# Layer norms' statistics, centred tokens and residual in two sets of SBUF buffers instead of columns of z's PSUM bank

## The chip, the cores and the metric

The kernel runs on one core of a Trainium2 chip. The core's engines are TensorE (PE, matrix products and transposes), VectorE (DVE), ScalarE (ACT), GpSimd (POOL) and SyncE (SP, which here only issues transfers); each runs its own queue in order and waits on semaphores. The metric is the device time of one execution in microseconds.

## What is computed

One layer of a small language model on 2 x 2048 tokens: a gather of 64 columns of an embedding table, a layer norm, a block of two selective scans (one forward, one backward in time), and a layer of 32 experts of which each token takes one. Cut to what matters:

```python
h = table[:, 192:256][x]                       # tokens 2 x 2048, 64 channels
a = attn(layernorm(h)); h = h + a              # attn normalises once more and adds its own input
h = h + experts(layernorm(h))

def attn(x):                                   # 64 channels in, 128 inside
    c, gate = split((layernorm(x) * g + b) @ in_w.T)
    act = silu(conv4(c))
    fwd, bwd = mamba(act), flip(mamba(flip(act)))
    return concat(fwd, bwd) * silu(gate) @ out_w.T + x

def mamba(u):                                  # per direction
    x, z = split(u @ in_w.T); x = silu(conv4(x))
    dt = softplus(...x...); B, C = 16 columns each of x @ xproj_w.T
    h_t = h_{t-1} * exp(dt * A) + dt * x * B;  y = sum_n h_t * C + x * D   # 16 states per channel
    return y * silu(z) @ out_w.T
```

## The kernel before

Tokens are cut into 8 chunks of 512. A *unit* is one chunk in one direction; there are 16, numbered 0 to 15, eight for each row of the batch (four forward, then four backward). A unit's scan has 16 states, held as four groups r = 0 to 3 of four quarters q, so a unit is 16 scans over 512 steps, at *places* p = 0 to 15 of the unit (r = p // 4). All engines run the loop `for u in range(UNITS)` in an order written out by hand: DVE and ACT have a function `between(u, p)` each, which says what stands behind scan or decay p; PE has one list per unit.

The work of a unit is divided as follows:

- ACT makes the decays exp(dt A) in three PSUM banks in turn (L979), at most three scans ahead of DVE, and the softplus (L955 to L968) of the unit two further on.
- DVE scans (L1336). It also forms the input products of groups 1 and 3, dt x times a row of B that PE spreads into a PSUM bank (L1323), each of 2048 columns.
- POOL forms the input products of groups 0 and 2 from SBUF operands (L454, called B(u,r) below), multiplies every group of scanned states by C, also from SBUF (L463, called C(u,r)), and ends the softplus of unit u+2 in three instructions (L440, L443, L447). All its operands are in SBUF. Its order in unit u is C(u-1,3), B(u,2), C(u,0), softplus, C(u,1), B(u+1,0), C(u,2). C(u,r) waits for scan 4r+3 of the unit (by the semaphore `scanned`), B(u+1,0) for PE's fold of C(u,0).
- PE folds the products by C into y (L639), spreads B, and does the other products.

Layer norms are done on DVE and ACT between scans. `norm_first`/`norm_sum` add up the channels (L1230); `norm_centre` subtracts the mean (L1234, into `xc`); ACT squares (L908, `sq`); `norm_var` sums the squares and forms the variance with one or two TENSOR_SCALARs (L1239 to L1242); ACT takes its logarithm and an exponential (L913, L915, into `lnr`); `norm_newton` corrects the inverse root in three small instructions (L1250 to L1252), each with a wait on the one before; `scaled` multiplies `xc` by it (L1255). Sums, squares, variance and Newton's values stand in columns 384 to 415 of PSUM bank `ZED`. There is one `xc`.

There are sixteen norms. Norms 0 to 7 are those of the gathered chunks; each has two results, `u2d` twice over (the input of the in-projection, `start_u2`) and the once-normed tokens, which `start_residual` builds in columns 0 to 255 of bank `ZED` and adds to `x0` (L1270). Norms 0 to 3 run in the prologue. Norm 4+k is begun at place 15 of unit k and goes on in unit k+1 (k = 0 to 3): `norm_var` at place 0, Newton and `start_u2` at place 1, `start_residual` at place 12. Norms 8 to 15 are those ahead of the experts, with the one result `xf`. Four are begun at place 15 of units 5, 7, 9, 11 (the table `ENDS`) and go on in units 6, 8, 10, 12; three (`QUICK`, chunks of units 12 to 14) run inside units 13 to 15; the last runs after the loop.

Bank `ZED` also takes, once per unit, PE's product z for three units ahead (`zed`, L592, read by ACT in L949), and the experts' logits. Therefore `norm_first` waits until ACT has read z (`z_ready`) and until the expert of the chunk before is chosen (`choice_ready`), and PE's `zed` waits for `u_added`.

## Time and profile before

| | |
|---|---|
| median of 3 runs | 615.37 us |
| lowest, highest | 614.62, 620.71 us |
| the profiled execution | 620.66 us, its span 618.9 us |
| POOL busy | 517.5 us (84%) |
| DVE busy | 484.0 us (78%) |
| PE busy, ACT busy | 451.6 us, 356.2 us |
| the 16 x 16 scans on DVE (L1336) | 235.1 + 78.1 us, 1267 ns each |
| POOL's products, by C and by B | 284.5 + 140.4 us, 4.53 us each |
| granted TensorE clock, mean | 0.817 |

The loop begins at about 80 us, and POOL's last product ends at 578; what follows is the last two chunks' experts, on PE, ACT and DVE. A timeline row gives an instruction's start from the span's start, its length and, in brackets, how long its engine had been idle before it and what released it. "x2" merges neighbours.

### The profile page before, as it was taken

What the parts mean: (1) busy time and instruction counts of PE and PEld (TensorE: products, weight loads), DVE (VectorE), ACT (ScalarE), POOL (GpSimd) and SP (SyncE); (2) the same over time, 40 slices, a digit from 0 to 9 for tenths busy, and PEclk for the clock granted to TensorE, in tenths of its full rate; (3) what the DMA queues carried; (4) which work ended last, traced back from release to release, by engine and by line L of the source; (5) the groups of instructions that cost most, each with busy time, mean ns of one, the idle gap of its engine ahead of it and who ended that gap; (6) DMA issues with size and microseconds to landing.
All of it is one profiled execution on the core that took longest, in us unless ns stands there. A gap on an engine that the chain in (4) does not pass through costs nothing.

```text
span 618.9 us, 5369 instructions
## 1 busy us (share of the span) xinstructions
PE 451.6 (73%) x1485; PEld 160.7 (26%) x1485; DVE 484.0 (78%) x600; ACT 356.2 (58%) x634; POOL 517.5 (84%) x190
## 2 busy tenths in 40 slices
PE   2476756577777777778796887777777765777887
PEld 1222212132222221313141323132313221323332
DVE  3433069898989897989699989898989898899720
ACT  2354565757575757474748494849484944555222
POOL 5727159999999999999989999999999999897100
PEclk9887957787878787869787987898779876879856
DMA  6829358846464646563716772667276726400000
GB/s 66 33 30 181 79 138 205 190 136 142 136 143 129 149 135 137 141 143 107 171 50 144 175 171 73 171 152 167 70 168 163 162 68 160 87 10 1 8 4 14
DMA packets 51072, 71.31 MB, mean 115 GB/s; under 512 B 16434, under 2 KB 17378, under 8 KB 51042
## 3 DMA queue, kind: packets, MB, share of 16 engines
q1 hardware_dynamic: 48050, 69.63, 46.6%
q0 software_dynamic: 1024, 1.05, 4.4%
q10 hardware_dynamic: 1968, 0.29, 0.3%
q8 instruction: 12, 0.20, 0.2%
q14 instruction: 18, 0.15, 0.1%
HBM read 60.45 MB, written 10.49 MB: 115 GB/s over the span
## 4 chain that ended last, share of the span: by engine, by line
POOL 38%; issue 26%; PE 17%; DVE 10%; ACT 5%; ACTq 1%; another core or an unknown queue 1%; POOLq 0%; DVEq 0%
POOL st L463 20%; POOL st L454 13%; DVE st L1336 5%; PE ps L725 3%; POOL l_ L440 2%; POOL dt L443 2%; DVE st L1323 2%; PE ps L741 2%; PE ps L639 2%; PE ps L579 2%; PE ps L651 1%; ACTq L893 1%; PE ps L626 1%; PE ps L558 1%; PE ps L724 1%
## 5 line engine op out<-in xcount | busy, mean ns | idle before, releaser
L463 POOL TENSOR_TENSOR st<-st,repC 128x2048 f32<-128x2048 f32 x63 | 284.5, 4526 | 10.3 <-ACT carry L985 7.0
L1336 DVE TENSOR_TENSOR_SCAN st<-ps,carry,st 128x512 f32<-128x512 f32 x192 | 235.1, 1267 | 20.1 <-ACT carry L985 12.0
L979 ACT ACTIVATE ps<-dtS,negA 128x512 f32<-128x512 f32 x256 | 169.1, 680 | 53.5 <-DVE st L1336 52.1
L454 POOL TENSOR_TENSOR st<-duS,repB 128x2048 f32<-128x2048 f32 x31 | 140.4, 4529 | 0.0
L639 PE MATMUL ps<-st,fold 128*32 128x512 f32 x504 | 83.7, 742 | 74.1 <-POOL st L463 74.0
L1336 DVE TENSOR_TENSOR_SCAN st<-ps,zero,st 128x512 f32<-128x512 f32 x64 | 78.1, 1266 | 3.1 <-ACT ps L979 2.9
L1323 DVE TENSOR_TENSOR st<-duS,ps 128x2048 f32<-128x2048 f32 x33 | 74.9, 2271 | 3.6 <-PE ps L626 3.2
L579 PE MATMUL ps<-act,wT 128*128 128x512 f32 x128 | 64.3, 648 | 5.2 <-issue 5.2
L985 ACT ACTIVATE carry<-st 128x4 f32<-128x4 f32 x48 | 9.8, 205 | 77.3 <-DVE st L1336 77.1
L626 PE MATMUL ps<-xr,Bw 128*128 128x512 f32 x66 | 48.9, 833 | 6.8 <-DVE lnr L1316 6.0
L440 POOL TENSOR_TENSOR l_<-l_,e_ 128x512 f32<-128x512 f32 x16 | 20.4, 1276 | 29.8 <-DVE e_ L1274 29.8
L639 PEld LDWEIGHTS ps<-st,fold 128*32 128x32 f32 x504 | 10.8, 117 | 122.7 <-POOL st L463 114.1
L428 POOL DMA_INDIRECT x<-in_L_tok_ple_table,idx x32 | 30.5, 952 | 12.5 <-issue 9.3
L725 PE MATMUL ps<-xfT,w 64*128 64x512 f32 x64 | 40.5, 718 | 0.0
L579 PEld LDWEIGHTS ps<-act,wT 128*128 128x128 f32 x128 | 26.2, 212 | 38.2 <-issue 37.4
L1012 ACT ACTIVATE tall<-ps,b 128x512 f32<-128x512 f32 x32 | 21.7, 678 | 22.0 <-PE ps L725 21.8
L609 PE MATMUL ps<-xr,wT 128*32 128x512 f32 x32 | 25.5, 893 | 11.5 <-DVE st L1323 11.4
L600 PE MATMUL ps<-xr,dtproj 128*128 128x512 f32 x32 | 23.3, 818 | 13.7 <-ACT xr L942 13.5
L1274 DVE SCALAR_TENSOR_TENSOR e_<-ps,e_ 128x512 f32<-128x512 f32 x16 | 10.7, 669 | 23.7 <-ACT l_ L968 23.7
L741 PE MATMUL ps<-tall,w 128*64 128x256 f32 x128 | 22.8, 516 | 8.3 <-ACT tall L1012 8.3
L651 PE MATMUL ps<-zr,wT 128*128 128x512 f32 x32 | 25.6, 892 | 1.2 <-DVE zr L1342 1.2
L884 ACT ACT_TABLE_LOAD x16 | 20.5, 1283 | 9.7 <-issue 9.5
(126 smaller groups left out, 579.4 us busy)
## 6 DMA issues: line engine op xcount, KB each, us to landing
dtS<-dt_dram SPq DMA_DIRECT2D x64, 256.0 KB, 7.2
duS<-du_dram SPq DMA_DIRECT2D x64, 256.0 KB, 4.8
repC<-bc_dram SPq DMA_DIRECT2D x64, 256.0 KB, 5.7
repB<-bc_dram SPq DMA_DIRECT2D x60, 128.0 KB, 2.8
dt_dram<-dt SPq DMA_DIRECT2D x16, 256.0 KB
du_dram<-du SPq DMA_DIRECT2D x16, 256.0 KB
bc_dram<-bc_sb SPq DMA_DIRECT2D x16, 64.0 KB, 5.5
out_h<-fin SPq DMA_DIRECT2D x8, 128.0 KB, 2.1
```

What stands on the lines that cost most here:

```text
L440: pool.tensor_tensor(l_[:], l_[:], e_[:], ALU.subtract).then_inc(sem("sp_log1p"), 1)
L454: pool.tensor_tensor(st[:, r], duS[:, u % 2], row, ALU.mult).then_inc(sem("dbu_pool"), 1)
L463: pool.tensor_tensor(st[:, r], st[:, r], row, ALU.mult).then_inc(sem("hc_ready"), 1)
L579: mm = pe.matmul(ps[:, bank, :], conv_wT(way(u), k), act_at(u, 6 - k if way(u) else k), start=(k == 0), stop=(k == 3))
L626: pe.matmul(ps[:, SHORT, :], Bw[:, way(u), r, :], x_of(u), start=True, stop=True) \
L639: mm = pe.matmul(ps[32 * q:32 * q + 32, Y, :], fold[:], st[:, r, q], start=False, stop=(r == NR - 1), skip_group_check=True)
L651: pe.matmul(ps[:, SHORT, :], wT[:, 12 + way(u), :], z_of(u), start=True, stop=True) \
L725: pe.matmul(ps[:, bank, :], w1[:, 8 * k:8 * k + 8, :].rearrange("p e h -> p (e h)"), xfT[0:DM, :], start=False, stop=True).then_inc(sem("h ...
L741: mm = pe.matmul(ps[DM * h:DM * h + DM, bank, 0:T // 2], w, src, start=(k == 0), stop=(k == NBLK), skip_group_check=True)
L979: sc.activation(decay_bank(u, r, q), dtS[:, u % 2, q], ACT.Exp, scale=negA[:, way(u), q, r:r + 1]).then_inc(sem("decay_ready"), 1)
L1323: dve.tensor_tensor(st[:, r], duS[:, u % 2], row, ALU.mult).then_inc(sem("dbu_dve"), 1)
L1336: dve.tensor_tensor_scan(st[:, r, q, order], decay_bank(u, r, q)[:, order], st[:, r, q, order], first, ALU.mult, ALU.add).then_inc(sem("sc ...
```

## The change

The statistics get an SBUF tile `stats` with two sets of 32 columns; `xc` and `lnr` (now `lnrs`) get two sets as well; norm n uses set n % 2. The once-normed tokens of chunks 0 to 7 are built in `fin`, the SBUF tile that the kernel's output leaves from later on. Bank `ZED` then no longer holds anything of a norm, and the waits for it go: DVE's on `z_ready` and `choice_ready`, PE's on `u_added`.

```diff
+        lnrs = sb("lnrs", [P, 2, 2, 2 * TC])
+        stats = sb("stats", [P, 2, 32])
-        xc = sb("xc", [P, TC, DM])
+        xc = sb("xc", [P, 2, TC, DM])
...
-        sum_ps = ps[:, ZED, 384:384 + TC]
-        ss_ps = ps[:, ZED, 388:388 + TC]
-        var_ps = ps[:, ZED, 392:400]
-        nt_ps = ps[:, ZED, 400:408]
-        ny_ps = ps[:, ZED, 408:416]
+        def stat(n, at, width):
+            return stats[:, n % 2, at:at + width]
...
             def zed(u, bank):
                 if bank == ZED:
-                    if norm_b(u - 3) is not None and norm_b(u - 3) < NCH:
-                        pe.wait_ge(sem("u_added"), norm_b(u - 3) + 1)
...
-                dve.scalar_tensor_tensor(xc[:], wide(sum_ps), -1.0 / DM, src, ALU.mult, ALU.add) \
+                dve.scalar_tensor_tensor(xc[:, n % 2], wide(stat(n, 0, TC)), -1.0 / DM, src, ALU.mult, ALU.add) \
...
-                    ch.step(dve.tensor_scalar(var_ps[:, TC:], ss_ps, (1.0 + EPS) / DM, EPS * EPS, ALU.mult, ALU.add))
+                    ch.step(dve.tensor_scalar(stat(n, 8 + TC, TC), stat(n, 4, TC), (1.0 + EPS) / DM, EPS * EPS,
+                                              ALU.mult, ALU.add))
...
-                ch.step(dve.tensor_tensor(nt_ps[:, 0:w], var_ps[:, 0:w], r, ALU.mult))
+                ch.step(dve.tensor_tensor(stat(n, 16, w), stat(n, 8, w), r, ALU.mult))
...
-            def scaled(dst, k):
-                return dve.scalar_tensor_tensor(dst, xc[:], -0.5, wide(ny_ps[:, TC * k:TC * k + TC]),
+            def scaled(n, dst, k):
+                return dve.scalar_tensor_tensor(dst, xc[:, n % 2], -0.5, wide(stat(n, 24 + TC * k, TC)),
...
-                ch.step(scaled(u_ps, 0))
+                ch.step(scaled(n, fin[:], 0))
                 src = x0_of(TC * n)
-                dve.tensor_tensor(src, u_ps, src, ALU.add).then_inc(sem("u_added"), 1)
+                dve.tensor_tensor(src, fin[:], src, ALU.add).then_inc(sem("u_added"), 1)
...
-                    dve.wait_ge(sem("z_ready"), n - CB + 4)
...
-                    wait(dve, "choice_ready", n - NCH)
-                    dve.wait_ge(sem("z_ready"), min(BEGINS[n - NCH] + 4, UNITS))
```

Beside that, the hand-written orders of DVE, ACT and PE are new in many places: on DVE the residual (p 12 to 1), `normed` of units 6, 8, 10, 12 (p 3 to 2), input product 3 (p 11 to 10), the expert's choice (p 6 and 7 to p 7 and 9), and in units 13 to 15 the centring (p 7 to 8) and Newton's step (p 12 to 11); on ACT the softplus (in p 0 to 1, its exponential and sum p 0 and 3 to 6, its logarithm p 4 to 7); on PE the folds and experts' products within the unit. POOL's and SP's queues are the same.

The same stretch of DVE's queue in unit 2, from Newton's step to the scans behind it; `st<-ps,carry,st` is a scan. Before:

```order
L1250 TENSOR_TENSOR ps<-ps,lnr 128x8
L1251 TENSOR_TENSOR ps<-ps,lnr 128x8
L1252 SCALAR_TENSOR_TENSOR ps<-ps,lnr 128x8
L1255 SCALAR_TENSOR_TENSOR u2d<-xc,ps 128x4x64 x2
L1336 SCALAR_TENSOR_TENSOR st<-ps,carry,st 128x512 x2
```

and the residual, ten scans later in the same unit:

```order
L1336 SCALAR_TENSOR_TENSOR st<-ps,carry,st 128x512
L1255 SCALAR_TENSOR_TENSOR ps<-xc,ps 128x256
L1270 TENSOR_TENSOR x<-ps,x 128x256
L1336 SCALAR_TENSOR_TENSOR st<-ps,carry,st 128x512 x3
```

The same place after the change (its `x<-fin,x` is the residual's add):

```order
L1250 TENSOR_TENSOR stats<-stats,lnrs 128x8
L1251 TENSOR_TENSOR stats<-stats,lnrs 128x8
L1252 SCALAR_TENSOR_TENSOR stats<-stats,lnrs 128x8
L1255 SCALAR_TENSOR_TENSOR u2d<-xc,stats 128x4x64 x2
L1255 SCALAR_TENSOR_TENSOR fin<-xc,stats 128x256
L1268 TENSOR_TENSOR x<-fin,x 128x256
L1334 SCALAR_TENSOR_TENSOR st<-ps,carry,st 128x512 x2
```

The operands called `ps` are now `stats` and `fin`, and the residual's two instructions moved ahead of the two scans.

DVE's queue in unit 13, from the norm's sum to the scans behind Newton's step, before:

```order
L1230 TENSOR_REDUCE ps<-x 128x4
L1234 SCALAR_TENSOR_TENSOR xc<-ps,x 128x256
L1336 SCALAR_TENSOR_TENSOR st<-ps,carry,st 128x512 x4
L1323 TENSOR_TENSOR st<-duS,ps 128x2048
L1239 TENSOR_REDUCE ps<-sq 128x4
L1242 TENSOR_SCALAR ps<-ps 128x4
L1336 SCALAR_TENSOR_TENSOR st<-ps,carry,st 128x512
L1250 TENSOR_TENSOR ps<-ps,lnr 128x4
L1251 TENSOR_TENSOR ps<-ps,lnr 128x4
L1252 SCALAR_TENSOR_TENSOR ps<-ps,lnr 128x4
L1336 SCALAR_TENSOR_TENSOR st<-ps,carry,st 128x512
L1255 SCALAR_TENSOR_TENSOR xf<-xc,ps 128x256
```

and with the change:

```order
L1229 TENSOR_REDUCE stats<-x 128x4
L1334 SCALAR_TENSOR_TENSOR st<-ps,carry,st 128x512 x2
L1233 SCALAR_TENSOR_TENSOR xc<-stats,x 128x256
L1334 SCALAR_TENSOR_TENSOR st<-ps,carry,st 128x512 x2
L1321 TENSOR_TENSOR st<-duS,ps 128x2048
L1238 TENSOR_REDUCE stats<-sq 128x4
L1242 TENSOR_SCALAR stats<-stats 128x4
L1334 SCALAR_TENSOR_TENSOR st<-ps,carry,st 128x512
L1250 TENSOR_TENSOR stats<-stats,lnrs 128x4
L1251 TENSOR_TENSOR stats<-stats,lnrs 128x4
L1252 SCALAR_TENSOR_TENSOR stats<-stats,lnrs 128x4
L1334 SCALAR_TENSOR_TENSOR st<-ps,carry,st 128x512 x2
```

The sum comes one scan earlier and the centring one scan later; the input product, the variance and Newton's step come one scan earlier, and the copy `xf` has two scans between Newton's step and itself instead of one.

## Rows read from the trace of the kernel before

**Rows 1.** The page: busy time by engine; then the chain that ended last, by engine.

```profile
PE 451.6 (73%) x1485; PEld 160.7 (26%) x1485; DVE 484.0 (78%) x600; ACT 356.2 (58%) x634; POOL 517.5 (84%) x190
...
POOL 38%; issue 26%; PE 17%; DVE 10%; ACT 5%; ACTq 1%; another core or an unknown queue 1%; POOLq 0%; DVEq 0%
```

**Rows 2.** Waits of all engines: who waited for whom, us in total, times, longest.

```profile
PEld ps L639 <- POOL st L463: 114.1, 49, 6.0
...
POOL l_ L440 <- DVE e_ L1274: 29.8, 3, 16.6
...
POOL st L463 <- ACT carry L985: 7.0, 3, 4.4
...
POOL st L494 <- DVE st L1336: 3.9, 1, 3.9
...
POOL st L463 <- DVE st L1336: 3.3, 2, 2.3
```

**Rows 3.** POOL's timeline (start us, us, instruction), units 1 and 2, and unit 7.

```profile
141.37 9.00 POOL L463 TENSOR_TENSOR st<-st,repC 128x2048 f32<-128x2048 f32 x2
150.34 4.53 POOL L454 TENSOR_TENSOR st<-duS,repB 128x2048 f32<-128x2048 f32 x1
154.82 4.52 POOL L463 TENSOR_TENSOR st<-st,repC 128x2048 f32<-128x2048 f32 x1
...
315.30 1.28 POOL L440 TENSOR_TENSOR l_<-l_,e_ 128x512 f32<-128x512 f32 x1 [1.84 <-DVE e_ L1274]
```

**Rows 4.** DVE's timeline (same columns), end of unit 1 and start of unit 2.

```profile
141.43 0.42 DVE L1234 SCALAR_TENSOR_TENSOR xc<-ps,x 128x256 f32<-128x256 f32 x1
143.44 1.28 DVE L1336 TENSOR_TENSOR_SCAN st<-ps,carry,st 128x512 f32<-128x512 f32 x1 [1.58 <-ACT ps L979]
...
145.39 2.29 DVE L1323 TENSOR_TENSOR st<-duS,ps 128x2048 f32<-128x2048 f32 x1
147.59 1.28 DVE L1336 TENSOR_TENSOR_SCAN st<-ps,carry,st 128x512 f32<-128x512 f32 x1
148.78 0.16 DVE L1250 TENSOR_TENSOR ps<-ps,lnr 128x8 f32<-128x8 f32 x1
...
149.39 0.87 DVE L1255 SCALAR_TENSOR_TENSOR u2d<-xc,ps 128x256 f32<-128x256 f32 x2
150.19 2.45 DVE L1336 TENSOR_TENSOR_SCAN st<-ps,carry,st 128x512 f32<-128x512 f32 x2
```

**Rows 5.** POOL's timeline, end of unit 7 and start of unit 8.

```profile
328.20 9.02 POOL L463 TENSOR_TENSOR st<-st,repC 128x2048 f32<-128x2048 f32 x2
337.16 4.54 POOL L454 TENSOR_TENSOR st<-duS,repB 128x2048 f32<-128x2048 f32 x1
341.64 4.54 POOL L463 TENSOR_TENSOR st<-st,repC 128x2048 f32<-128x2048 f32 x1
```

**Rows 6.** DVE's timeline, end of unit 7 and scans of unit 8.

```profile
329.28 0.42 DVE L1234 SCALAR_TENSOR_TENSOR xc<-ps,x 128x256 f32<-128x256 f32 x1
...
338.50 0.40 DVE L1255 SCALAR_TENSOR_TENSOR xf<-xc,ps 128x256 f32<-128x256 f32 x1
```

**Rows 7.** DVE's line 1476 by duration, min/median/max; then POOL's timeline beside it.

```profile
L1476 DVE TENSOR_TENSOR st<-st,repC x3: 679/679/1576, 577.2 to 579.3; 128x512 f32<-128x512 f32 x3
...
576.94 1.28 POOL L494 TENSOR_TENSOR st<-st,repC 128x512 f32<-128x512 f32 x1 [3.90 <-DVE st L1336]
```

**Rows 8.** DVE's groups at the start, each shape apart: busy us, mean ns.

```profile
L1198 DVE TENSOR_TENSOR st<-st 32x128 f32<-32x128 f32 x1 | 0.3, 280 | 0.0
L1197 DVE TENSOR_SCALAR st<-st 32x128 f32<-32x128 f32 x1 | 0.2, 218 | 0.0
```

**Rows 9.** POOL's timeline in unit 13.

```profile
508.69 4.54 POOL L454 TENSOR_TENSOR st<-duS,repB 128x2048 f32<-128x2048 f32 x1
513.18 9.00 POOL L463 TENSOR_TENSOR st<-st,repC 128x2048 f32<-128x2048 f32 x2
```

**Rows 10.** POOL's timeline, first softplus.

```profile
42.21 1.27 POOL L440 TENSOR_TENSOR l_<-l_,e_ 128x512 f32<-128x512 f32 x1 [11.37 <-DVE e_ L1274]
```

More of the change, by code:

```diff
@@ L816, in _ @@
                     partial(u - 1)
+                if 1 <= u <= CB:
+                    x_chunk(CB + u - 1, LONG)
+                if third:
+                    experts_out(ENDS[u - 2])
                 if u - 2 in QUICK:
@@ L837, in _ @@
                 if u - 2 in QUICK:
-                    experts_out(u - 2)
+                    hidden(u - 2, 3)
+                if second:
+                    turn_choice(ENDS[u - 1])
+                if u + 3 < UNITS:
+                    zed(u + 3, ZED)
                 if third:
                     turn_back(ENDS[u - 2])
-                if u + 3 < UNITS:
-                    zed(u + 3, ZED)
+                if u - 2 in QUICK:
+                    experts_out(u - 2)
                 if 1 <= u <= CB:
@@ L907, in squares @@
                 sc.wait_ge(sem("centred"), n + 1)
-                sc.activation(sq[:], xc[:], ACT.Square).then_inc(sem("squared"), 1)
+                sc.activation(sq[:], xc[:, n % 2], ACT.Square).then_inc(sem("squared"), 1)
             def rsqrt(n):
@@ L1065, in between @@
                         keep_last(u, 0)
+                if p == 6:
+                    if u + 2 < UNITS:
+                        softplus_exp(u + 2)
+                    if u + 2 < UNITS:
+                        softplus_plus1(u + 2)
                     if u - 2 in ENDS:
                         hidden_relu(ENDS[u - 2], 3)
-                if p == 6:
+                    if 1 <= u <= CB:
+                        uT_chunk(CB + u - 1)
+                if p == 7:
+                    if u + 2 < UNITS:
+                        softplus_ln(u + 2)
                     if u - 1 in ENDS:
@@ L1238, in norm_var @@
                 dve.wait_ge(sem("squared"), n + 1)
-                ch.step(dve.tensor_reduce(ss_ps, sq[:], AX, ALU.add))
+                ch.step(dve.tensor_reduce(stat(n, 4, TC), sq[:], AX, ALU.add))
                 if n < NCH:
-                    ch.step(dve.tensor_scalar(var_ps[:, TC:], ss_ps, (1.0 + EPS) / DM, EPS * EPS, ALU.mult, ALU.add))
-                dve.tensor_scalar(var_ps[:, 0:TC], ss_ps, 1.0 / DM, EPS, ALU.mult, ALU.add) \
+                    ch.step(dve.tensor_scalar(stat(n, 8 + TC, TC), stat(n, 4, TC), (1.0 + EPS) / DM, EPS * EPS,
+                                              ALU.mult, ALU.add))
+                dve.tensor_scalar(stat(n, 8, TC), stat(n, 4, TC), 1.0 / DM, EPS, ALU.mult, ALU.add) \
                    .then_inc(sem("ln_var"), 1)
@@ L1406, in between @@
                         input_product(u, 1)
-                    if is_unit(u) and 2 in on_dve(u):
-                        input_product(u, 2)
                     if u - 2 in QUICK:
@@ L1484, in _ @@
             norm_first(NCH + nth(last), x0_of(tile0(last)))
-            norm_centre(x0_of(tile0(last)))
+            norm_centre(NCH + nth(last), x0_of(tile0(last)))
             norm_var(NCH + nth(last))
```

151 lines of the change are left out of this document (69 added, 82 removed).

## The prediction

> **What bounds the kernel now.** I read four views. The page comes first: POOL is busy for 517.5 us and DVE for 484.0 us of 618.9, and the chain that ended last runs for 38% of the span through POOL, more than through any other engine [rows 1]. POOL's own waits come next: 29.8 us ahead of the softplus, of which only 1.84 us lie inside the loop (at 315.30, in unit 7), and 7.0, 3.9 and 3.3 us, all in the first unit and the last two [rows 2, 3]. POOL's timeline shows the same thing from inside: in units 1 to 13 each instruction starts where the last one ends, 4.5 us apart: the pair at 141.37 fills 9.00 us and B(2,2) follows at 150.34 [rows 3]. So whatever makes POOL idle in those units is lost for good. DVE's timeline, last, shows how little room there is: in unit 2 its scan number 3 ends at 152.6 and POOL takes the product that needs it, C(2,0), at 154.82 [rows 3, 4]. In unit 8 the pair is 338.5 and 341.64 [rows 5, 6]. DVE leads POOL by two to three microseconds, no more.
>
> **A look at what DVE's operands are.** In the loop of the kernel before, no DVE instruction reads two tensors from SBUF: one of the two is always in PSUM. The one exception stands after the loop: L1476, SBUF times SBUF. Its three instances take 679, 679 and 1576 ns; the first starts at 577.2 and the last at 579.3, so the long one is the first (two short ones ahead of it would put the last at 578.6). It starts while POOL's L494 (also SBUF times SBUF) runs from 576.94 to 578.22. It ends at 578.8, some 0.55 us after POOL's; the two behind it meet an idle POOL and take 679 [rows 7]. My reading: a DVE instruction with two SBUF inputs is held until the POOL instruction that is reading SBUF has ended.
>
> **The change part by part.** Every norm's intermediate moves to SBUF. These DVE instructions now have two SBUF inputs: the centring, the three of Newton's step, and each scaled copy (one for the experts' norms; two for u2d, one and the add for the residual of chunks 4 to 7). A norm's TENSOR_SCALARs now go from SBUF to SBUF with one input. The nearest rows are at the start: an immediate TENSOR_SCALAR on 32x128 in SBUF takes 218 ns, the two-input TENSOR_TENSOR of the same size 280 [rows 8]. It gets through its columns in less time than one input stream gives the other, so I take it to use the second input path too, and to be held. POOL's instructions in the loop all read SBUF and take 4.5 us. I work out three kinds of norm against the old time axis; what counts is when the next POOL instruction that needs a scan can start.
>
> *Chunks 4 to 7, units 1 to 4.* In unit 2 the centring arrives at 141.43, with POOL in C(1,2), and then the two TENSOR_SCALARs, each with a wait on the one before. The first ends with C(1,3) at 150.34, the second with B(2,2) at 154.82 [rows 3, 4]. C(2,0) needs four scans, so POOL now stands still and nothing holds DVE any longer. Behind the second TENSOR_SCALAR lie the product 2.2, a scan 1.2, Newton 0.6, u2d 0.8, the residual, which the change moves here from later in the unit, 0.8 (two instructions of u2d's size), and two scans 2.4: 8.0, with the TENSOR_SCALAR itself 8.2 us, by which C(2,0) is late [rows 4]. Four units: 33. If one-input instructions are not held, the first wait is Newton's, to the same 154.82, and 0.6 + 0.8 + 0.8 + 2.4 = 4.6 is left, or 18 for four.
>
> *Experts' norms in units 6, 8, 10, 12.* In unit 8 the centring (329.28) waits for C(7,2), the TENSOR_SCALAR for C(7,3) to 337.16, then 3.4 for product and scan, and Newton's first waits for B(8,2), to 341.64 [rows 5, 6]. After it: Newton 0.6, a scan 1.2, the xf copy 0.4 (moved up one scan), a scan 1.2: C(8,0) is 3.4 late. Four units: 14.
>
> *Units 13 to 15.* The centring stands one scan later than before, Newton's step behind scan 11. By then both B(14,0) and C(13,2) are ready for POOL, so its first instruction ends with B at 513.18 and its second with C(13,2) at 517.67; four scans and the xf copy, 5.4, then hold up C(13,3) [rows 9]. In unit 14 the same gives about 4.4, since POOL idles already. In unit 15 POOL works with gaps and DVE is the bound, so each hold counts: about 4 at the centring and 4 at Newton's. Sum 18.
>
> *Prologue.* Chunk 2's norm meets the three 1.27 us instructions of the first softplus, from 42.21 on, at its TENSOR_SCALARs and at Newton's step; it loses two of their lengths, 2.5 [rows 10]. The gathers that stand around it are no compute instructions; I cost them at nothing, and up to 5 if they hold DVE as well. The last norm runs when POOL has finished: nothing.
>
> *What I cost at nothing.* The waits that are dropped (on z, on the expert's choice, PE's on u_added) stood ahead of a POOL that never paused, so their going frees nothing that sets the end. The new order on PE is covered by its 114.1 us of waits for POOL's products [rows 2]. One place there is a new wait: in units 1 to 4 the transposes of u2d now stand ahead of the fold of C(u-1,3). If u2d is late, that fold and DVE's y times z behind it are late too; in between lie the residual and two scans, 3.2 us, for four transposes and one fold, and I take that as enough. ACT's softplus moves from places 0 to 4 to places 1 to 7, nearer to the DVE step that POOL waits for ahead of its own softplus. POOL waited there once in the loop, 1.84 us [rows 3]; where the cover is gone I allow as much again in each of units 1 to 4, 7 us for the upper bound, and nothing in the sum. An operand in SBUF instead of PSUM saves little: xf, written to SBUF, takes 0.40, and the centring 0.42 [rows 6]. SP's queue is the same.
>
> **The sum.** 33 + 14 + 18 + 2.5 = 67.5, of which 15 hang on the one-input instructions (without them 53). The profiled execution took 620.66 us (span 618.9), the median of the runs is 615.37; I add to the median: 683 us, or 668 without them. Either side of that, leads that DVE rebuilds and holds that find POOL idle make 655 to 705.
>
> The Trainium skill (SBUF — State Buffer, section "Who interferes with whom") says this outright: a DVE instruction with two SBUF inputs contends with a GpSimd one that reads SBUF, as does a tensor_scalar in its two-port mode, and the second to issue blocks until the first ends. The trace agrees with its 1576 ns against 679. By that rule the sum is the higher one of the two above; by the 1576 ns alone, a row that shows no one-input instruction beside POOL, it is the lower one.
>
> **Rivals.**
> *DVE starves.* POOL's next instruction starts before the last is quite over: the pair at 141.37 ends at 150.37, B(2,2) starts at 150.34 [rows 3]. If it takes its turn ahead of the held DVE instruction, DVE waits until POOL runs dry. Then unit 2's centring goes at 154.82, and 10.3 us of DVE's work (from 141.43 to 152.6, less its idle 1.58, plus the residual) [rows 4] lie before C(2,0): 41 for four; unit 8 gives 9, 36 for four; units 13 to 15 give 6.3 + 5.5, some 36. With the prologue 115: 730 us. For it: POOL's density. Against: nothing in the trace shows who wins. Chance 0.12.
> *No hold to speak of.* The 1576 ns have another cause (L1476 is also the first after fin, and its operand had just been written), or a hold lasts only for a part of a long instruction. Then all is covered as above, and the time is 615, between 613 and 620. For it: one instance is thin. Chance 0.17, of which 0.14 within 1% and 0.03 a little slower by ACT's and PE's new orders.
> *Faster.* Nothing holds, and the earlier norms and PE's new order close POOL's gaps, 1.84 in unit 7 and the 7.0, 3.9 and 3.3 of the first and last units, 16 in all [rows 2, 3], for 599 us. It decides if over 6.2 of them are won. Against: the gaps end with a scan or its carry, and DVE is not relieved of any work. Chance 0.04.
>
> **How the numbers follow.** Held by the instruction, 0.67, with 683 as its time and 655 to 705 as its own range. Within 1% (about what a measurement of this kernel can tell from no change) 0.14, faster 0.04, slower 0.82. The range leaves out the last two rivals, 0.21 less the little of them that ends above 640, and reaches to the starving case: 640 to 735.
>
> **What would show it.** Right: Newton's instructions of 0.17 us recorded at up to 4.5 us, ending at the end of a POOL instruction; POOL gaps of 8 us before C(u,0) in units 1 to 4, and of 3 to 4 in 6, 8, 10, 12; none in 7, 9, 11. TENSOR_SCALARs on stats of 4 us or of 0.17 tell 683 from 668. Wrong: those instructions at 0.2 us throughout, or POOL still gapless. DVE holds that span two or three POOL instructions mean the starving case.

## The result, and the profile after

The changed kernel takes 696.92 us (median of 4 runs, 688.86 to 698.19) where the kernel before, on the same chip, takes 617.88 (614.62 to 620.71): ratio 1.125, 95% interval 1.114 to 1.137, 79 us slower. The prediction was 683 us, range 640 to 735. The profiled execution took 697.75 us, its span 695.9 against 618.9, so 77.0 us are to be found in the trace. The mean granted clock went from 0.817 to 0.755. The ratios here and below leave out executions that took over 1.5% longer than the quickest of their kernel.

The page of after, busy time by engine and the chain that ended last (before: [rows 1]):

```profile
PE 475.3 (68%) x1485; PEld 166.7 (24%) x1485; DVE 578.1 (83%) x600; ACT 360.4 (52%) x634; POOL 519.9 (75%) x190
...
DVE 46%; PE 25%; issue 14%; ACT 10%; DMA 2%; another core or an unknown queue 1%; POOL 1%; DVEq 0%; ACTq 0%
```

DVE is busy for 94.1 us more with the same 600 instructions, POOL for 2.4 us more. The chain that ran for 38% through POOL now runs for 46% through DVE and for 1% through POOL. PE's 23.7 us more, for the same 1485 products, stand beside the lower clock. Neither makes the loss: the stretch behind POOL's last product, where PE has most of the work, went from 40.7 to 35.2 us, and experiment B has a kernel as slow with only 1.6 us more on PE.

DVE's groups by shape (busy us, mean ns, idle before). With their operands in PSUM the same instructions took 424 (centring), 170 (both TENSOR_SCALARs) and about 170 ns (Newton's):

```profile
L1233 DVE SCALAR_TENSOR_TENSOR xc<-stats,x 128x256 f32<-128x256 f32 x16 | 38.6, 2410 | 0.4
L1242 DVE TENSOR_SCALAR stats<-stats 128x4 f32<-128x4 f32 x16 | 34.9, 2180 | 0.6
L1240 DVE TENSOR_SCALAR stats<-stats 128x4 f32<-128x4 f32 x8 | 13.9, 1736 | 0.3
L1251 DVE TENSOR_TENSOR stats<-stats,lnrs 128x4 f32<-128x4 f32 x8 | 9.9, 1242 | 0.3
...
L1255 DVE SCALAR_TENSOR_TENSOR xf<-xc,stats 128x256 f32<-128x256 f32 x8 | 8.0, 994 | 0.0
...
L1238 DVE TENSOR_REDUCE stats<-sq 128x4 f32<-128x256 f32 x16 | 6.4, 402 | 3.2 <-ACT sq L908 3.2
...
```

An instruction over four columns takes 2180 ns in the mean. The reductions, also from SBUF to SBUF, take what they took. The time stands in the instructions' own length, and not in idle time ahead of them: the wait is inside the instruction. A wait of this kind is called a *hold* below.

What POOL waits for (before: [rows 2]):

```profile
POOL st L465 <- ACT carry L985: 62.8, 22, 8.4
...
POOL l_ L442 <- DVE e_ L1272: 38.3, 14, 18.1
POOL st L465 <- DVE st L1334: 17.3, 3, 8.1
```

Ahead of its products by C (L465) POOL waits 62.8 + 17.3 us instead of 7.0 + 3.3. The carry is ACT's copy of a scan's last column, so both rows mean a late scan. The softplus (L442) waited 3 times, now 14.

**Unit 2 close up.** POOL's timeline (before: [rows 3]), then DVE's (before: [rows 4]):

```profile
149.03 4.52 POOL L465 TENSOR_TENSOR st<-st,repC 128x2048 f32<-128x2048 f32 x1
154.52 4.52 POOL L465 TENSOR_TENSOR st<-st,repC 128x2048 f32<-128x2048 f32 x1 [0.97 <-ACT carry L985]
159.00 4.50 POOL L456 TENSOR_TENSOR st<-duS,repB 128x2048 f32<-128x2048 f32 x1
171.85 4.52 POOL L465 TENSOR_TENSOR st<-st,repC 128x2048 f32<-128x2048 f32 x1 [8.36 <-ACT carry L985]
```

```profile
149.49 4.34 DVE L1233 SCALAR_TENSOR_TENSOR xc<-stats,x 128x256 f32<-128x256 f32 x1
153.75 1.27 DVE L1334 TENSOR_TENSOR_SCAN st<-ps,carry,st 128x512 f32<-128x512 f32 x1
...
155.37 3.70 DVE L1240 TENSOR_SCALAR stats<-stats 128x4 f32<-128x4 f32 x1
159.10 4.42 DVE L1242 TENSOR_SCALAR stats<-stats 128x4 f32<-128x4 f32 x1
163.43 2.27 DVE L1321 TENSOR_TENSOR st<-duS,ps 128x2048 f32<-128x2048 f32 x1
...
166.83 0.13 DVE L1250 TENSOR_TENSOR stats<-stats,lnrs 128x8 f32<-128x8 f32 x1
...
168.65 0.42 DVE L1268 TENSOR_TENSOR x<-fin,x 128x256 f32<-128x256 f32 x1
168.99 2.45 DVE L1334 TENSOR_TENSOR_SCAN st<-ps,carry,st 128x512 f32<-128x512 f32 x2
```

Each long instruction ends with a POOL instruction. The centring, from 149.49 to 153.83, ends 0.28 us behind the product by C of 149.03, which ends at 153.55. The first TENSOR_SCALAR ends at 159.07 with the product of 154.52 (159.04). The second ends at 163.52 with the product by B of 159.00 (163.50). Then POOL has nothing to run until scan 3 is done at 171.4, and nothing is held: Newton's first takes 0.13 us, the residual's add 0.42. That is 8.36 us of gap, and what DVE does in it, unheld, is on the path.

**Unit 8 close up.** POOL's timeline and DVE's (before: [rows 5, 6]):

```profile
370.41 9.14 POOL L465 TENSOR_TENSOR st<-st,repC 128x2048 f32<-128x2048 f32 x2
379.52 4.51 POOL L456 TENSOR_TENSOR st<-duS,repB 128x2048 f32<-128x2048 f32 x1
387.69 4.52 POOL L465 TENSOR_TENSOR st<-st,repC 128x2048 f32<-128x2048 f32 x1 [3.65 <-ACT carry L985]
```

```profile
371.13 4.05 DVE L1233 SCALAR_TENSOR_TENSOR xc<-stats,x 128x256 f32<-128x256 f32 x1
...
376.72 2.87 DVE L1242 TENSOR_SCALAR stats<-stats 128x4 f32<-128x4 f32 x1
...
382.89 1.17 DVE L1250 TENSOR_TENSOR stats<-stats,lnrs 128x4 f32<-128x4 f32 x1
```

Three holds, to 375.18, 379.59 and 384.06; the last ends with POOL's product by B (384.03), and C(8,0) is 3.65 us late.

### The profile page after: what moved, and what is told of

The parts are those of the page before. It is cut to its first block, busy times and chain, and to the rows that moved or that the text cites. A ratio compares the mean times of both kernels' runs of the same rounds, so it can differ in the third digit from the quotient of the medians.

```text
span 695.9 us, 5362 instructions
## 1 busy us (share of the span) xinstructions
PE 475.3 (68%) x1485; PEld 166.7 (24%) x1485; DVE 578.1 (83%) x600; ACT 360.4 (52%) x634; POOL 519.9 (75%) x190
## 4 chain that ended last, share of the span: by engine, by line
DVE 46%; PE 25%; issue 14%; ACT 10%; DMA 2%; another core or an unknown queue 1%; POOL 1%; DVEq 0%; ACTq 0%
DVE st L1334 24%; DVE st L1321 7%; DVE xc L1233 3%; PE ps L581 3%; PE ps L725 3%; PE ps L639 2%; PE ps L741 2%; ACT ps L979 2%; DVE stats L1240 2%; PE ps L626 2%; PE ps L651 2%; ACT L884 2%; PE ps L660 2%; DMA x<-in_L_tok_ple_table,idx 2%; DVE stats L1251 1%
## 5 line engine op out<-in xcount | busy, mean ns | idle before, releaser
L465 POOL TENSOR_TENSOR st<-st,repC 128x2048 f32<-128x2048 f32 x63 | 285.7, 4541 | 80.3 <-ACT carry L985 62.8
L979 ACT ACTIVATE ps<-dtS,negA 128x512 f32<-128x512 f32 x256 | 173.1, 684 | 95.8 <-DVE st L1334 95.2
L639 PE MATMUL ps<-st,fold 128*32 128x512 f32 x504 | 111.4, 877 | 35.1 <-POOL st L465 34.9
L581 PE MATMUL ps<-act,wT 128*128 128x512 f32 x128 | 65.7, 660 | 5.4 <-ACT act L930 5.4
L609 PE MATMUL ps<-xr,wT 128*32 128x512 f32 x32 | 26.9, 938 | 50.7 <-DVE st L1321 50.7
L442 POOL TENSOR_TENSOR l_<-l_,e_ 128x512 f32<-128x512 f32 x16 | 20.3, 1271 | 38.3 <-DVE e_ L1272 38.3
L725 PE MATMUL ps<-xfT,w 64*128 64x512 f32 x64 | 42.4, 749 | 0.0
L430 POOL DMA_INDIRECT x<-in_L_tok_ple_table,idx x32 | 30.8, 961 | 12.6 <-issue 9.3
L1233 DVE SCALAR_TENSOR_TENSOR xc<-stats,x 128x256 f32<-128x256 f32 x16 | 38.6, 2410 | 0.4
L639 PEld LDWEIGHTS ps<-st,fold 128*32 128x32 f32 x504 | 14.0, 128 | 90.8 <-POOL st L465 48.1
L1242 DVE TENSOR_SCALAR stats<-stats 128x4 f32<-128x4 f32 x16 | 34.9, 2180 | 0.6
L1012 ACT ACTIVATE tall<-ps,b 128x512 f32<-128x512 f32 x32 | 21.8, 681 | 16.4 <-PE ps L725 16.2
L741 PE MATMUL ps<-tall,w 128*64 128x256 f32 x128 | 20.4, 466 | 13.8 <-ACT tall L1012 13.8
L600 PE MATMUL ps<-xr,dtproj 128*128 128x512 f32 x32 | 20.4, 723 | 11.3 <-ACT xr L942 11.3
```

Source lines behind the costliest of these rows:

```text
L465: pool.tensor_tensor(st[:, r], st[:, r], row, ALU.mult).then_inc(sem("hc_ready"), 1)
L581: mm = pe.matmul(ps[:, bank, :], conv_wT(way(u), k), act_at(u, 6 - k if way(u) else k), start=(k == 0), stop=(k == 3))
L639: mm = pe.matmul(ps[32 * q:32 * q + 32, Y, :], fold[:], st[:, r, q], start=False, stop=(r == NR - 1), skip_group_check=True)
L725: pe.matmul(ps[:, bank, :], w1[:, 8 * k:8 * k + 8, :].rearrange("p e h -> p (e h)"), xfT[0:DM, :], start=False, stop=True).then_inc(sem("h ...
L979: sc.activation(decay_bank(u, r, q), dtS[:, u % 2, q], ACT.Exp, scale=negA[:, way(u), q, r:r + 1]).then_inc(sem("decay_ready"), 1)
L1233: dve.scalar_tensor_tensor(xc[:, n % 2], wide(stat(n, 0, TC)), -1.0 / DM, src, ALU.mult, ALU.add) \
```

## The experiments

**A. Which kinds of instruction are held.** The kernel before, with one tiny instruction added at each of six moments at which POOL runs; a single execution, 616.35 us against 614.69.

```diff
+            def probe(u, p):
+                if (u, p) == (5, 9):
+                    dve.tensor_tensor(po[:, 0:4], pd[:, 0:4], pd[:, 4:8], ALU.mult)
+                if (u, p) == (7, 9):
+                    dve.tensor_scalar(po[:, 4:8], pd[:, 0:4], 2.0, 1.0, ALU.mult, ALU.add)
+                if (u, p) == (9, 9):
+                    dve.tensor_scalar(po[:, 8:12], pd[:, 0:4], pd[:, 60:61], pd[:, 61:62], ALU.mult, ALU.add)
+                if (u, p) == (9, 13):
+                    dve.tensor_scalar(po[:, 12:13], pd[:, 0:1], 2.0, 1.0, ALU.mult, ALU.add)
+                if (u, p) == (11, 9):
+                    dve.tensor_copy(po[:, 16:20], pd[:, 0:4])
+                if (u, p) == (11, 13):
+                    dve.tensor_reduce(po[:, 20:24], pd[:, 0:32].rearrange("p (a b) -> p a b", b=8), AX, ALU.add)
```

> The kernel before with six small DVE instructions added in units that have no norm, each on SBUF tiles of its own, each behind a scan and beside a POOL product of 4.5 us: in unit 5 a TENSOR_TENSOR with two SBUF inputs, in 7 a TENSOR_SCALAR with immediates on four columns, in 9 a TENSOR_SCALAR with pointer scalars and one on a single column, in 11 a copy of four columns and a TENSOR_REDUCE. My theory: the TENSOR_TENSOR, the immediate TENSOR_SCALAR and the copy are held to the end of POOL's running instruction (0.2 to 4.5 us each), the reduction is not (0.2 us); the pointer and single-column forms are open. Rival, only two tensor inputs are held: the TENSOR_SCALAR and the copy take 0.1 to 0.2 us. Rival, no port but something in the norms: all six at 0.2 us. Time: at most 5 us above the kernel before.

The six on DVE's timeline, with POOL's instruction of the moment behind the first, the third, the fourth and the fifth:

```profile
252.76 1.17 DVE L1472 TENSOR_TENSOR po<-pd 128x4 f32<-128x4 f32 x1
252.65 1.26 POOL L445 TENSOR_TENSOR dt<-v_,l_ 128x512 f32<-128x512 f32 x1
...
314.64 0.95 DVE L1474 TENSOR_SCALAR po<-pd 128x4 f32<-128x4 f32 x1
...
376.33 0.91 DVE L1476 TENSOR_SCALAR po<-pd 128x4 f32<-128x4 f32 x1
375.95 1.27 POOL L445 TENSOR_TENSOR dt<-v_,l_ 128x512 f32<-128x512 f32 x1
...
384.19 0.13 DVE L1478 TENSOR_SCALAR po<-pd 128x1 f32<-128x1 f32 x1
383.01 4.53 POOL L456 TENSOR_TENSOR st<-duS,repB 128x2048 f32<-128x2048 f32 x1
...
437.88 1.00 DVE L1480 COPY po<-pd 128x4 f32<-128x4 f32 x1
437.59 1.26 POOL L445 TENSOR_TENSOR dt<-v_,l_ 128x512 f32<-128x512 f32 x1
...
445.83 0.16 DVE L1482 TENSOR_REDUCE po<-pd 128x4 f32<-128x32 f32 x1
```

The two-input one ends at 253.93, POOL's at 253.91; the TENSOR_SCALAR with scalars from memory at 377.24, POOL's at 377.22; the copy at 438.88, POOL's at 438.85. All four kinds over four columns are held, one input or two. A TENSOR_SCALAR over one column (128 ns) and a reduction (161 ns) are not, each in the middle of a 4.5 us POOL instruction. Each case is one instance; for the reduction, the 32 of the changed kernel (402 and 411 ns in the mean, from SBUF to SBUF) say the same.

**B. The holds or the new orders.** First all tiles in SBUF with the hand-written orders of before, then the tiles in PSUM with the new orders. The first applies every hunk of the diff that is shown ahead and none of the orders:

```diff
+        lnrs = sb("lnrs", [P, 2, 2, 2 * TC])
+        stats = sb("stats", [P, 2, 32])
...
-                ch.step(scaled(u_ps, 0))
+                ch.step(scaled(n, fin[:], 0))
```

> The changed kernel's buffers (statistics, xc, residual in SBUF, the waits on z gone) with the orders of DVE, ACT and PE as they were before. If the holds make the 77 us, this is as slow or nearly: 670 to 700 us, with DVE's norm instructions ending at the end of POOL's. The residual at place 12 then takes its own holds, so units 1 to 4 may lose more than 10 us each. If the new orders make it, 615 to 630 us.

The second applies only the orders, on DVE, ACT and PE, such as

```diff
-                if u + 2 < UNITS:
-                    pre(u + 2)
-                if u - 2 in QUICK:
-                    turn_normed(u - 2)
                 if is_unit(u):
                     b_rows(u, 1)
+                if u - 2 in QUICK:
+                    turn_normed(u - 2)
+                if u + 2 < UNITS:
+                    pre(u + 2)
```

> The kernel before, with its statistics in the PSUM bank and its waits, in the new orders of DVE, ACT and PE. If the holds make all of the loss: 610 to 620 us, with POOL gapless. In the changed kernel units 5, 7, 9, 11 and 13, which I had expected without a gap, have POOL gaps of 0.5 to 2.4 us; if the new order makes these, this kernel shows them too and takes 624 to 630 us.

SBUF with the old orders: 700.29 us against 614.69, ratio 1.143 (1.135 to 1.152), DVE busy 590.7. PSUM with the new orders: 620.88 against 614.69, ratio 1.011 (1.003 to 1.019), DVE busy 483.0. So the tiles make the loss, and the new orders by themselves add 6.2 us to the kernel before (by the interval, 2 to 12); the kernel with SBUF tiles is no slower with them (696.92 us, ratio 1.125) than without (700.29, ratio 1.143). The first also settles whether a slower PE makes the loss: its PE is busy for 453.2 us, 1.6 more than before. Its trace shows where the time goes: with the residual at place 12, in the middle of POOL's work, its two instructions are held as well.

```profile
143.47 3.33 DVE L1256 SCALAR_TENSOR_TENSOR fin<-xc,stats 128x256 f32<-128x256 f32 x1
146.83 4.63 DVE L1269 TENSOR_TENSOR x<-fin,x 128x256 f32<-128x256 f32 x1
...
146.48 4.70 POOL L465 TENSOR_TENSOR st<-st,repC 128x2048 f32<-128x2048 f32 x1
156.46 4.50 POOL L465 TENSOR_TENSOR st<-st,repC 128x2048 f32<-128x2048 f32 x1 [5.29 <-ACT carry L985]
```

DVE's two rows of unit 1, then POOL's: the hold moves to C(1,3), which starts 5.29 us late, and from C(1,0) to C(4,0) a unit takes 43.7 to 44.4 us instead of the 40.3 to 41.0 of the new order and 30.8 before. In the new order the residual stands where POOL is already idle. In the second kernel POOL is gapless in units 5 to 13; in units 2 to 4 it has gaps of 0.62, 0.95 and 0.77 us ahead of the softplus and of 1.07 ahead of C(4,0), and units 2 and 3 take 31.8 and 32.9 us.

**C. TENSOR_SCALARs with their scalars in SBUF.** In the changed kernel, a try at an unheld form.

```diff
-                    ch.step(dve.tensor_scalar(stat(n, 8 + TC, TC), stat(n, 4, TC), (1.0 + EPS) / DM, EPS * EPS,
+                    ch.step(dve.tensor_scalar(stat(n, 8 + TC, TC), stat(n, 4, TC), kv[:, 0:1], kv[:, 1:2],
                                               ALU.mult, ALU.add))
-                dve.tensor_scalar(stat(n, 8, TC), stat(n, 4, TC), 1.0 / DM, EPS, ALU.mult, ALU.add) \
+                dve.tensor_scalar(stat(n, 8, TC), stat(n, 4, TC), kv[:, 2:3], kv[:, 3:4], ALU.mult, ALU.add) \
```

> The changed kernel, with the variance's TENSOR_SCALARs taking their two constants from an SBUF tile, one per partition, instead of as immediates; same results. If only the immediate form uses the second input path, they fall from up to 4.4 us to 0.2, Newton's first instruction takes over the wait, C(u,0) in units 1 to 4 is 4.6 us late instead of 8.2, and the time falls by some 15 us to 682. If the pointer form is held as well, or the holds do not come from the path, no change: 697.

694.33 us against 614.69, ratio 1.132 (1.124 to 1.141), with the same gap of 8.36 us before C(2,0) and DVE busy 578.5: nothing changes, as the 911 ns of experiment A say. The form of the scalars is not what decides.

**D. The variance on ACT.** In the changed kernel, ACT scales and adds, and no TENSOR_SCALAR is left in the norm.

```diff
-                sc.wait_ge(sem("ln_var"), n + 1)
+                sc.wait_ge(sem("ss_ready"), n + 1)
+                if n < NCH:
+                    sc.activation(stat(n, 8 + TC, TC), stat(n, 4, TC), ACT.Identity, scale=(1.0 + EPS) / DM,
+                                  bias=kv[:, 1:2]).then_inc(sem("ln_var"), 1)
+                sc.activation(stat(n, 8, TC), stat(n, 4, TC), ACT.Identity, scale=1.0 / DM,
+                              bias=kv[:, 0:1]).then_inc(sem("ln_var"), 1)
+                sc.wait_ge(sem("ln_var"), min(2 * n + 2, n + 1 + NCH))
```

> The changed kernel with the variance (scale and offset) computed on ACT instead of by DVE's TENSOR_SCALARs; results the same up to rounding. It takes 48.8 us of DVE's time (4.1 of them unheld) away. By the prediction's rule Newton's first instruction takes over the wait: C(u,0) in units 1 to 4 is 4.6 late instead of 8.2, units 6, 8, 10, 12 stay: 683 us. If all of DVE's held time counts, and only part of it passes on to Newton: 660 to 680. If holds do not matter there: 697.

684.00 us against 617.06, ratio 1.112 (1.104 to 1.120). The gap before C(2,0) is 4.92 us instead of 8.36, those before C(3,0) and C(4,0) are 4.65 and 4.92; those of units 6 to 12 stay at 3.45 to 3.65. DVE in unit 2:

```profile
159.50 4.38 DVE L1254 TENSOR_TENSOR stats<-stats,lnrs 128x8 f32<-128x8 f32 x1 [0.43 <-ACT lnrs L922]
163.92 0.17 DVE L1255 TENSOR_TENSOR stats<-stats,lnrs 128x8 f32<-128x8 f32 x1
```

Newton's first, never held in this unit of the changed kernel, now is, for the same 4.4 us that the TENSOR_SCALAR was held. An instruction that is taken away leaves its place in the queue of holds to the next one. Taking it away gains only the work that stood between the two.

**E. The residual alone in SBUF.** The kernel before, with the once-normed tokens in `fin` instead of bank `ZED`, at place 12 as before. PE's wait on `u_added`, which the change drops, is kept.

```diff
-                ch.step(scaled(u_ps, 0))
+                ch.step(scaled(fin[:], 0))
                 src = x0_of(TC * n)
-                dve.tensor_tensor(src, u_ps, src, ALU.add).then_inc(sem("u_added"), 1)
+                dve.tensor_tensor(src, fin[:], src, ALU.add).then_inc(sem("u_added"), 1)
```

> The kernel before with one part of the change alone: the residual of chunks 0 to 7 is built in fin (SBUF), all else in PSUM, old order. Its add then has two SBUF inputs and is held once in each of units 1 to 4, at place 12, for up to 4.3 us, the copy ahead of it is not. By the lead rule: 615 to 617. If DVE has no room: 4 x 4 less 3 to 6, so 624 to 628.

633.87 us against 617.06, ratio 1.030 (1.023 to 1.037): 16.8 us, where 615 to 617 was expected if DVE's lead covers the holds and 624 to 628 if not. Four of the eight adds meet POOL; DVE's row, then two of POOL's:

```profile
137.21 4.58 DVE L1270 TENSOR_TENSOR x<-fin,x 128x256 f32<-128x256 f32 x1
...
137.00 4.52 POOL L454 TENSOR_TENSOR st<-duS,repB 128x2048 f32<-128x2048 f32 x1
...
149.14 4.55 POOL L463 TENSOR_TENSOR st<-st,repC 128x2048 f32<-128x2048 f32 x1 [2.98 <-ACT carry L985]
```

The eight adds take 16.4 us instead of 3.4, so 13.0 us of holding, and POOL's gaps in units 1 to 4 add up to some 14.5. But these gaps are not what a hold costs by itself. Scan 15 of unit 1 ends at 145.34, and POOL's product ahead of C(1,3) at 146.17, so a late scan alone would have cost C(1,3) nothing. POOL waits for ACT's carry copy. The held add posts `u_added`, PE's z waits for that, ACT waits for z, and the copy stands behind it in ACT's queue:

```profile
141.85 2.08 PE L592 MATMUL ps<-act,wT 128*128 128x512 f32 x2 [4.18 <-DVE x L1270]
...
144.02 0.60 ACT L949 ACTIVATE zr<-ps 128x512 f32<-128x512 f32 x1 [3.85 <-PE ps L592]
...
148.81 0.19 ACT L985 ACTIVATE carry<-st 128x4 f32<-128x4 f32 x1
```

The same ACT instruction waits 2.54, 2.08 and 2.53 us for PE in units 2 to 4. So the run prices a hold together with a wait that the changed kernel no longer has.

**F. POOL's products in halves.** In the changed kernel each 128x2048 product of POOL's is two of 128x1024.

```diff
-                pool.tensor_tensor(st[:, r], st[:, r], row, ALU.mult).then_inc(sem("hc_ready"), 1)
+                pool.tensor_tensor(st[:, r, 0:2], st[:, r, 0:2], row[:, 0:2], ALU.mult)
+                pool.tensor_tensor(st[:, r, 2:4], st[:, r, 2:4], row[:, 2:4], ALU.mult).then_inc(sem("hc_ready"), 1)
```

> The changed kernel with each of POOL's products in two instructions of 1024 columns instead of one of 2048; the work is the same. If a held DVE instruction waits for the end of POOL's running instruction, no hold is longer than 2.3 us, DVE's held time falls from 94 to some 50 us and the time to 655 to 672 us, POOL's own overhead for the extra instructions (0.1 to 0.4 each, of which it has 6 per unit) among it. If the length of POOL's instruction has no part in it: 697 to 710.

689.86 us against 617.06, ratio 1.121 (1.114 to 1.129); 655 to 672 was expected. Half of that came true: no hold is longer than 2.35 us. But there are more of them.

```profile
157.59 2.27 DVE L1244 TENSOR_SCALAR stats<-stats 128x4 f32<-128x4 f32 x1
...
L1253 DVE TENSOR_TENSOR stats<-stats,lnrs 128x4 f32<-128x4 f32 x8 | 14.0, 1755 | 0.3
L1254 DVE SCALAR_TENSOR_TENSOR stats<-stats,lnrs 128x4 f32<-128x4 f32 x8 | 13.9, 1741 | 0.3
```

The first row is on DVE's timeline of unit 2, the others are groups. The eight each of Newton's second and third took 9.9 and 1.3 us in all in after; at 370.44 and 372.75, for one, each now ends with another half of B(8,2). DVE is busy for 558.2 us, only 19.9 less than in after, and POOL for 534.3, 14.4 more, since two halves take longer than a whole. The length of POOL's instruction sets a hold's length; what a norm loses is set by how many instructions meet a busy POOL.

**G. A dose of holds in the kernel before.** One tiny two-input instruction a unit, in units 5 to 12, first behind scan 12, then behind scan 2.

```diff
                     scan(u, p // NQ, p % NQ)
+                    if 5 <= u <= 12 and p == 12:
+                        dve.tensor_tensor(po[:, u], pd[:, 0:4], pd[:, 4:8], ALU.mult)
                     between(u, p)
```

(the second kernel has `p == 2`.)

> The kernel before with one small TENSOR_TENSOR (two SBUF inputs, 128x4) behind scan 12 in each of units 5 to 12, where POOL is in B(u+1,0): in unit 8 from 355.7 to 359.0 on the old axis, so a hold of about 3.3 us each, 26 in all. By the rule of my prediction (only what makes the next POOL product late in that unit counts; the lead is rebuilt) nothing is lost: C(8,3) starts at 363.5, 4.2 after its scan; 615 us. If DVE, with its waits for ACT, is as tight as POOL over two units, the holds pile up once the lead is gone: 26 less some 8 to 10 of lead and slack, 630 to 635 us.

> The kernel before with the same small TENSOR_TENSOR (two SBUF inputs, 128x4) in units 5 to 12, but behind scan 2 instead of scan 12. In units 6, 8, 10 and 12 it meets B(u,2) just after its start and is held for some 4.3 us; scan 3 follows it, and C(u,0) needs scan 3: 1.3 us late, by the rule of my prediction, four times. In units 5, 7, 9, 11 it meets the end of C(u-1,3): 0.5 us, no loss. So 18 to 20 us held, as in the run at place 12 (19.4), and gaps of 1.3 before C(6,0), C(8,0), C(10,0), C(12,0), 5 in all: 620 to 623 us. If the lead that is gone is not rebuilt, further gaps of 0.5 to 1 follow in the same and the next unit, as in the changed kernel: 624 to 630. If the place has no part in it: what place 12 gave, one gap of 1 us every second unit.

Behind scan 12: 625.38 us against 617.06, ratio 1.016 (1.009 to 1.023). The eight are held for 19.4 us over what they take by themselves, and POOL's gaps for it are 0.93, 0.89 and 0.91 us ahead of products and 1.07 and 1.08 ahead of the softplus: 4.9 us in all. The median grew by 8.3 (by the ratio's interval, 6 to 14). So a quarter of the 19.4 us is found again in POOL's gaps and, by the interval, between a third and three quarters in the time.

Behind scan 2: 616.53 against 616.07, ratio 1.002 (0.998 to 1.006), no change. That ratio rests on eight of eleven executions; the other three took 624.81 to 630.78 us, while none of the 13 of the kernel before took over 618.18, and what sets them apart is not shown. The trace seemed to contradict the ratio, with 19.4 us in the eight instructions and five gaps of 1.1 to 1.7 us, but the profiled execution is one of the three (624.81 us, clock 0.815). A further execution of the same kernel:

> The kernel before with one tiny two-input SBUF instruction behind scan 2 of units 5 to 12, looked at once more. In the trace at hand, of an execution that took 624.8 us where the median of the kernel is 616.5, the eight instructions were held for 17.9 us over what they take by themselves, and POOL stood still for 7 us ahead of its second product by C in five units. If the median execution is different because its instructions meet POOL at other moments, this one shows shorter holds, 5 to 12 us in all, and POOL gaps of 2 us or less in all. If the holds are as long and the gaps are as large as before, the execution takes some 624 again and the difference to the median is chance.

This execution took 611.07 us (clock 0.849). DVE's row in unit 7 of the one and of the other, and POOL's product behind it in the first:

```profile
304.13 4.45 DVE L1475 TENSOR_TENSOR po<-pd 128x4 f32<-128x4 f32 x1
...
310.21 4.52 POOL L465 TENSOR_TENSOR st<-st,repC 128x2048 f32<-128x2048 f32 x1 [1.65 <-DVE st L1339]
```

```profile
302.57 1.18 DVE L1475 TENSOR_TENSOR po<-pd 128x4 f32<-128x4 f32 x1
```

Here the eight take 6.8 us in all, and POOL has no gap in units 1 to 13. In the first trace DVE comes to the instruction just after POOL's product began (304.05) and is held for nearly all of it; in the second, 1.2 us before POOL's instruction ends. So the eight instructions of one kernel take 19.4 or 6.8 us in all by where the two queues happen to stand. Why the queues stood differently is not shown.

**H. The two halves of the change.** Everything of the changed kernel, but with the experts' norms (8 to 15) back in bank `ZED` with their waits; and the same for norms 0 to 7 and the residual instead.

```diff
         def stat(n, at, width):
+            if n >= NCH:
+                return ps[:, ZED, 384 + at:384 + at + width]
             return stats[:, n % 2, at:at + width]
...
                     dve.wait_ge(sem("x0_added"), LASTS[n - NCH] + 1)
+                    wait(dve, "choice_ready", n - NCH)
+                    dve.wait_ge(sem("z_ready"), min(BEGINS[n - NCH] + 4, UNITS))
```

> The changed kernel, but the norms ahead of the experts (8 to 15) have their statistics in the columns of z's PSUM bank again, with the waits that belong to them; norms 0 to 7 stay in SBUF. If what is lost in units 5 to 13 is that stretch's own holds, only the prologue's 1.7 us and the 34.7 us of units 1 to 4 stay: 653 us, with no gap of POOL over 1 us in units 6 to 13, and centring, variance and Newton of the experts' norms at 0.42, 0.17 and 0.17 us. If DVE carries a lost lead out of units 1 to 4 and that makes the 10 us of small gaps in units 5 to 13 that the prediction did not have, those 10 stay too: 663.

(the other has `if n < NCH`, DVE's wait on `z_ready`, PE's on `u_added`, and the residual in the bank.)

> The other half: norms 0 to 7 and the residual back in z's PSUM bank with their waits, the experts' norms in SBUF. If the two halves are independent, this one gives the kernel before plus 24.4 (units 5 to 13) plus 16.2 (units 13 to the end) plus some 4 us for the new order in units 2 to 4: 662 us, and POOL's gaps of 3.5 to 3.7 us ahead of C(6,0), C(8,0), C(10,0), C(12,0) are there with the small ones beside them. If the small gaps came from units 1 to 4, they are gone and it gives 652.

With the experts' norms in PSUM: 656.99 us against 617.95, ratio 1.070 (1.056 to 1.084). POOL's gaps in units 1 to 4 are those of after (4.92, 8.36, 8.09, 8.36), and in units 5 to 13 it has none. With the first norms in PSUM: 663.13, ratio 1.081 (1.066 to 1.095); the gaps before C(6,0), C(8,0), C(10,0) and C(12,0) are 3.46, 3.65, 3.65 and 3.65, as in after. Expected were 653 and 662. POOL's rows say that the halves are independent. The times agree: 39.0 and 45.2 over before are 84.2; the new orders are in both, so their 6.2 are taken off once, which leaves 78.0, against 79.0 for the whole. That it comes within 1 us is luck, since each ratio's interval spans some 9 us either way. The small gaps of units 5 to 13 belong to those units' own holds and are not carried over from units 1 to 4.

No version was faster than the kernel before.

## Why the prediction was right, and where it was off

**The mechanism** is shown. In the loop, the long instructions of the norms end just behind a POOL instruction's end, those over four or eight columns by 0.02 to 0.03 us, those over 128x256 by 0.28 to 0.29, the same kinds are short where POOL is idle (0.13 and 0.42 us in unit 2), and holds alone, put into the kernel before, bring them back (A, E, G). *No hold to speak of* (615) and *faster* (599) fell.

**TENSOR_SCALARs.** The prediction took them to be held, on the strength of 218 ns against 280 [rows 8], and put 15 us on it. They are held: 2180 and 1736 ns, and experiment A. Their price was read too: taken off DVE altogether, they give back 12.9 us (696.92 to 684.00).

**DVE starves (730)** fell. Had POOL's next instruction always gone first, the centring of unit 2 would have lasted until POOL ran dry; it lasted 4.34 us. Two TENSOR_SCALARs in a row were held for 3.70 and 4.42 us, each to the end of one POOL instruction: DVE gets its turn at each end. POOL even pays a little for it: the pair at 370.41 takes 9.14 us, where the one at 328.20 took 9.02 [rows 5]. Over the whole kernel its 63 products by C take 1.2 us more (4541 ns in the mean instead of 4526).

**The sum, term by term, against the 77.0 us of span.** Ahead of the loop: 2.5 predicted, 1.7 found (C(0,0) at 95.0 instead of 93.2). Units 1 to 4, to the start of C(4,0): 33 predicted, 34.7 found. The 8.2 us a unit was 8.36, 8.09 and 8.36 in units 2 to 4. In unit 1 it was 4.92: there the centring came just ahead of the end of a POOL instruction (0.86 us instead of 4.3), so that each later hold ended one POOL instruction earlier; the last one was that of Newton's first (1.17 us, to the end of B(1,2)), and the product and the scan already lay ahead of it. What unit 1 fell short was made up, by luck, by what had been costed at nothing: gaps of 0.77 to 0.94 us ahead of the softplus in each of the four units (the allowance for the upper bound was 1.84 each) and of 0.97 us ahead of C(1,3) and C(2,3). Of the softplus gaps, those of units 2 to 4 stand with 0.62 to 0.95 us in the second kernel of B too, which has no holds. Those ahead of C(u,3) come from the centring: its hold in unit 2's norm ends at 153.83, ACT squares its result before it copies the carry (154.19), and C(1,3), which needs the carry, starts at 154.52. Units 13 to the end: 18 predicted, 16.2 found, and this is near by luck. Units 13, 14 and 15 lose 6.5, 7.8 and 7.5 us, where 5.4, 4.4 and 8 were predicted, and the stretch behind POOL's last product is 5.5 us shorter, which the prediction did not have. It is as short (35.1 us) in the kernel of H that holds the experts' norms, and 40.6 in the other.

**Units 5 to 13, from C(4,0) to C(13,0): 14 predicted, 24.3 found. This step failed.** Its four gaps were right: 3.4 predicted each, 3.46, 3.65, 3.65 and 3.65 found, 14.4 in all. What was wrong is "none in 7, 9, 11", and with it the thought that DVE rebuilds its lead between two norms. Two units of each kernel, from C(8,0) to C(10,0) (columns: length, busy us of PE, PE's weight loads, DVE, ACT and POOL with their instructions, clock, share of DMA, GB/s); before, then after:

```profile
341.64:403.30 61.66, 47.49 (x173) 16.50 (x172) 55.21 (x59) 40.50 (x73) 61.35 (x19) 0.86 0.61 147
```

```profile
387.69:456.36 68.67, 51.49 (x172) 17.77 (x172) 63.00 (x59) 41.32 (x73) 61.49 (x18) 0.76 0.57 131
```

DVE's busy time grows by 7.8 us and the two units by 7.0. DVE had been idle for 6.5 us of 61.7, in waits for ACT and PE, and is idle for 5.7 of 68.7: those waits stand at fixed places of the unit and hardly shrink when DVE is late. So here DVE, not POOL, sets the pace, and holds that the sum left out because POOL was not made late by them at once (at the centring, at the first TENSOR_SCALAR) come through as gaps of 0.31 to 1.28 us ahead of the softplus, of C(u,3), of C(9,0) and of C(13,0). They are 10.5 us in all, where the same stretch had one gap of 1.84 before. H shows that all but the 0.77 ahead of unit 4's softplus come with the holds of these units' own norms. One by one their paths are not shown, and not all run through a late scan: ahead of C(9,3) POOL waits 0.97 us for ACT's carry copy, behind the square of the tokens whose centring was held until 443.02, and starts at 443.72.

Should one price a hold in full, then? No run says so. In G 19.4 us of holds made 4.9 us of gaps and 8.3 us of time. In E 13.0 us made some 14.5 of gaps, but by way of PE's wait for the held add. What decides is who waits for the held instruction and for what stands behind it, on ACT and PE as well as on POOL, and whether DVE has an idle stretch between the hold and the next scan that POOL needs. The dose behind scan 12 has one, the wait for ACT's carry of up to 2.4 us at the first scan of the next unit. This reading fits the rows, but no run tested it alone.

**The rest of the difference.** Terms make 77.0 instead of 67.5; the median grew by 2.0 us more than the span, and the median of before itself came out 2.5 us above the one that the prediction added to. That is 683 to 697.

**The page of the skill** (Trainium skill, SBUF — State Buffer, section "Who interferes with whom") was, beside the 218 ns of rows 8, the prediction's ground for 683 rather than 668, and the traces agree with it in that both kinds of instruction are held; the two-port mode that the page names is itself seen in no row. They also show held a TENSOR_SCALAR with scalars from memory (911 ns) and one over as few as four columns.
